# Building the edge matrix of a graph layer in ten blocks of 64 destinations instead of five of 125

## The chip, the core and the metric

The kernel runs on one core of a Trainium2 chip, in one launch. The metric is the time of that launch on the device, in microseconds (us). TensorE multiplies, VectorE (DVE in the profile), ScalarE (ACT) and GpSimd (POOL) work on elements, SyncE (SP) issues most DMAs. Each engine works through its own queue in order and meets the others only through semaphores. A name such as DVEq stands for the queue side of an engine: loading registers from memory, register arithmetic, branches and waits.

## The reference

```python
dst = jnp.minimum((625 * uniform(10000) ** 2.0).astype(int32), 9999)   # then sorted; src follows
edge_index = jnp.stack([src, dst])
xn = _layernorm(x, axis=-1)
x = x + _L0_gnn_ref(xn, edge_index, edge_type_2, ...) + _L0_mix_ref(xn[None], ...)[0]
x = x + _L0_ffn_ref(...)[0]
xn = _layernorm(x, axis=-1)
x = x + _L1_gnn_ref(xn, batch0, edge_index, ...) + _L1_mix_ref(xn[None], ...)[0]
x = x + _L1_ffn_ref(...)[0]
```

There are 625 nodes of 512 features and 10,000 edges of two relations. The change concerns one early stage: from `src`, `dst` and `edge_type_2` the kernel makes a dense matrix of edge counts for each relation, sources by destinations, with which the graph layers later multiply. Since `dst` is the square of a uniform number and sorted, low destinations have many more edges than high ones.

## The kernel before

The edges lie as 80 tiles of 125 edges. For one edge tile VectorE makes two one-hot matrices in 16-bit floats: `oh_src` (125 edges by 625 sources, the `tensor_scalar` of L1171) and `oh_dst` (125 edges by 250 columns, L1172: 125 destinations of relation 0 and 125 of relation 1). TensorE multiplies one by the other (L1712). Destinations are cut in five blocks `j` of `P` = 125; a block has four banks of results (relation 0 and 1, source halves of 312 and 313), so each edge tile takes four matmuls, which accumulate in these banks.

An edge tile is only visited in a block to which it has edges. `EU` = 4 tiles make a group; VectorE first counts which groups each block needs (`pres`, a matmul of ones into the bank `rng`, then small reductions on one partition) and writes first group and number of groups for each block into `rng_i`. VectorE and TensorE then both load these numbers into registers (`value_load`, L1164, L1165 and L1707) and run a loop over groups (`Fori`, L1168 and L1708), written out for the four tiles in it.

The two engines meet in a ring. Each block parity has `EU` slots of `oh_src` and `oh_dst`. VectorE waits for `oh_used{j}` before it writes a slot, and TensorE waits for `oh_ready{j}`; so within a block VectorE can be `EU` tiles ahead. To begin with, the slots of block j+1 are given free when TensorE clears the banks of block j with matmuls of zeros (L1700).

After its loop TensorE closes the banks (L1716). Behind blocks 1, 2 and 3 it does the transposes of the normalised rows (L1650: 16, 16 and 8 matmuls). ScalarE copies the banks into `AT` with a sum for the node degrees (L676). Behind the last block TensorE goes on with the first big product of the mixer (stage `kq`, L1643), and VectorE with the 120 scale-and-add passes over the weight bases (`sum_bases`, L1183 and L1186), which wait for the last block. All order in this stage is written by hand; no planner decides any of it. In the changed kernel the lines of the stage are numbered some 12 higher.

Of the kernel before, what the change touches and what calls it, by code (L numbers as in the profile page):

```python
# [8 lines left out]
P = 125  # L9
# [3 lines left out]
EU = 4  # L13
# [29 lines left out]
PSUM_ORDER = [("rng", 1), ("A0", 8), ("hTa", 4), ("A2", 4), ("hTb", 1), ("xnTa", 3), ("A3", 4), ("xnTb", 2), ("A", 4),  # L43
# [27 lines left out]
A_BLOCK = [("A0", 0), ("A0", 4), ("A2", 0), ("A3", 0), ("A", 0)]  # L71
# [41 lines left out]
def gps_two_layers(nc, I, out):  # L113
# [3 lines left out]
    with ctx:  # L117
# [30 lines left out]
        rng_i = sb("rng_i", [1, 16], i32)  # L148
# [81 lines left out]
        oh_dst = [[ring[:, 876 * u + 626:876 * u + 876] for u in range(EU)] for ring in (oh, oh2)]  # L230
        iota_src = oh[:, 876 * EU:876 * EU + N]
        iota_dst = oh[:, 876 * EU + 626:876 * EU + 876]
        srcf = small[0:P, 0:ET]
        keyf = small[0:P, ET:ET * (1 + TT)].rearrange("p (j t) -> p j t", j=TT)
        dstf, relf = small[0:P, 480:560], small[0:P, 560:640]
        pres, gez = (tmp[0:P, i, 0:TT * ET // 2].bitcast(f16).rearrange("p (j t) -> p j t", j=TT) for i in range(2))
        rank2, held2 = (tmp[0:1, i, 256:256 + 2 * TT * EG].rearrange("p (i j q) -> p i j q", i=2, j=TT) for i in range(2))
        rg = small[0:1, 640:960]
# [301 lines left out]
        def _(pool):  # L540
            step = [0]

            def link(ins):
# [5 lines left out]
            pool.iota(rank2[:, 0, :, :], pattern=[[0, TT], [1, EG]], base=1, channel_multiplier=0, allow_small_or_imprecise_dtypes=True)  # L549
            pool.iota(rank2[:, 1, :, :], pattern=[[0, TT], [-1, EG]], base=EG, channel_multiplier=0, allow_small_or_imprecise_dtypes=True)  # L550
# [22 lines left out]
            pool.iota(iota_dst, pattern=[[1024, 2], [1, P]], base=0, channel_multiplier=0,  # L573
                      allow_small_or_imprecise_dtypes=True).then_inc(S("consts"), 1)
# [75 lines left out]
        def _(act):  # L650
# [46 lines left out]
            def adjacency_out(j):  # L697
                stage, n = A_BLOCK[j]
                for q in range(4):
                    r, (a, w) = q // 2, HALF[q % 2]  # L700
                    copy_out(stage, n + q, AT[:, r, j, a:a + w], B(stage, n + q)[0:P, 0:w], accum_out=deg_part[:, j, q:q + 1])

            adjacency_out(0)
            adjacency_out(1)
# [14 lines left out]
            adjacency_out(2)  # L719
# [3 lines left out]
            adjacency_out(3)  # L723
            for j in range(2):
                xn_columns("xnTb", j, 3 + j)
            adjacency_out(4)
# [320 lines left out]
        def _(dve):  # L1047
# [84 lines left out]
            dve.tensor_copy(pres[:, TT - 1, :], gez[:, TT - 1, :])  # L1132
            dve.tensor_tensor(pres[:, 0:TT - 1, :], gez[:, 0:TT - 1, :], gez[:, 1:TT, :], ALU.subtract).then_inc(S("presence"), 1)
# [5 lines left out]
            rr = rg[:, 0:TT * EG].rearrange("p (j q) -> p j q", j=TT)  # L1139
            rt2 = rg[:, 200:210]  # L1140
            groups_of, first_of = rt2[:, 0:TT], rt2[:, TT:2 * TT]
            most = rg[:, 210:220]
            last, back = most[:, 0:TT], most[:, TT:2 * TT]
# [12 lines left out]
            dve.tensor_copy(rng_i[0:1, 0:10], rt2).then_inc(S("ranges"), 1)  # L1156
# [6 lines left out]
            for j in range(TT):  # L1163
                groups = dve.value_load(rng_i[0:1, j:j + 1], min_val=1, max_val=EG)  # L1164
                q0 = dve.value_load(rng_i[0:1, 5 + j:6 + j], min_val=0, max_val=EG - 1)  # L1165
                if j > 1:
                    dve.wait_ge(S("psum_full"), filled(A_BLOCK[j - 2][0], A_BLOCK[j - 2][1] + 4))
                with dve.Fori(0, groups) as i:  # L1168
                    for u in range(EU):
                        dve.wait_ge(S(f"oh_used{j}"), EU * i + u + 1)  # L1170
                        dve.tensor_scalar(oh_src[j % 2][u], iota_src, small[0:P, bass.ds(EU * q0 + EU * i + u, 1)], None, ALU.is_equal)  # L1171
                        dve.tensor_scalar(oh_dst[j % 2][u], iota_dst, small[0:P, bass.ds(EU * q0 + EU * i + (ET * (j + 1) + u), 1)], None,  # L1172
                                          ALU.is_equal).then_inc(S(f"oh_ready{j}"), 1)
# [465 lines left out]
        def _(pe):  # L1639
# [52 lines left out]
            bk = claim(pe, "rng")  # L1692
            pe.wait_ge(S("presence"), 1)
            group(bk[0:1, 0:TT * ET], [(ones16[0:P, 0:1], pres.rearrange("p j t -> p (j t)"))]).then_inc(S("psum_full"), 1)
            for j in range(TT):
                stage, n = A_BLOCK[j]
                parts = [(B(stage, n + q), q // 2, HALF[q % 2]) for q in range(4)]
                for q, (bkq, r, (a, w)) in enumerate(parts):
                    claim(pe, stage, n + q)
                    ins = pe.matmul(bkq[0:P, 0:w], zero[:, 0:P], zero[:, 0:w], start=True, stop=False)  # L1700
                    if j < TT - 1:
                        ins.then_inc(S(f"oh_used{j + 1}"), 1)
                    if j == 0:
                        pe.matmul(bkq[0:P, 0:1], zero[:, 0:P], zero[:, 0:1], start=False, stop=False).then_inc(S("oh_used0"), 1)
                if j == 0:
                    pe.wait_ge(S("ranges"), 1)
                groups = pe.value_load(rng_i[0:1, j:j + 1], min_val=1, max_val=EG)  # L1707
# [7 lines left out]
                for bkq, r, (a, w) in parts:  # L1715
                    pe.matmul(bkq[0:P, 0:1], zero[:, 0:P], zero[:, 0:1], start=False, stop=True).then_inc(S("psum_full"), 1)  # L1716
# [516 lines left out]
```

## Time and profile before

| what | value |
|---|---|
| median of 3 runs | 808.13 us (807.37 to 809.75) |
| the profiled execution's own time | 807.63 us |
| its span in the profile | 805.9 us |
| TensorE busy | 783.2 us, 97% of the span |
| VectorE busy | 632.0 us, 78% |
| ScalarE busy | 293.2 us, 36% |
| mean granted clock of TensorE | 0.986 of full |

The profiled execution's time is 1.7 us more than its span, for what lies before the first and after the last instruction. Busy times of an engine are of overlapping instructions taken together once; the mean of one matmul is longer than the distance between two, since they are pipelined.

### The profile page before, as it was taken

To read this page: it belongs to the slowest core of one execution; us is meant where nothing else is said; L and a number is where in the kernel's file an instruction comes from. 1 tells how busy PE (TensorE), PEld (TensorE's weight loads), DVE (VectorE), ACT (ScalarE), POOL (GpSimd) and SP (SyncE) were. 2 spreads that over 40 slices of the span, in tenths; PEclk is the share of its full clock that TensorE was granted. 3 is DMA by queue.
4 is the path that set the end of the run, shared out by engine and by line. 5 is a ranking of instruction groups with operands and counts; after the bars stand their busy time and mean duration, and the time that the engine had idled before them with its cause. 6 is when DMAs were issued, how large, how long until landed. Compare 5 with 4: busy or idle time off the path is not lost.

```text
span 805.9 us, 10950 instructions
## 1 busy us (share of the span) xinstructions
PE 783.2 (97%) x3899; PEld 623.4 (77%) x3899; DVE 632.0 (78%) x918; ACT 293.2 (36%) x545; POOL 67.3 (8%) x74
## 2 busy tenths in 40 slices
PE   5999999999999999999999999999999999999997
PEld 4998757867477777477776878897898888888886
DVE  6867999999999999994968454338778865886863
ACT  4453214235411013124142633123445544545541
POOL 3100010220200000000401260030000000000000
PEclk9999999998999999999999999999799999999999
DMA  7600779796898786622041130008133231133101
GB/s 252 239 1 34 228 235 333 247 280 211 249 293 290 245 274 239 229 85 105 0 167 37 70 105 1 1 2 209 53 117 100 71 105 53 53 105 106 53 1 64
DMA packets 68268, 111.67 MB, mean 139 GB/s; under 512 B 4305, under 2 KB 21582, under 8 KB 68220
## 3 DMA queue, kind: packets, MB, share of 16 engines
q1 hardware_dynamic: 62426, 100.51, 37.5%
q0 software_dynamic: 2880, 5.12, 3.7%
q10 hardware_dynamic: 2914, 5.41, 1.8%
q8 instruction: 29, 0.48, 0.2%
q14 instruction: 19, 0.16, 0.1%
HBM read 107.18 MB, written 1.28 MB: 135 GB/s over the span
## 4 chain that ended last, share of the span: by engine, by line
PE 90%; DVE 6%; issue 2%; ACT 1%; DVEq 1%; DMA 0%; SPq 0%; ACTq 0%
PE bank L1643 54%; PE bank L2110 11%; PE bank L1712 6%; PE bank L1862 4%; PE bank L1881 3%; PE bank L1874 2%; PE bank L1855 2%; PE bank L1969 2%; PE bank L1650 2%; PE bank L1761 1%; PE bank L2044 0%; DVE ew_lo L1514 0%; DVE slot L1589 0%; DVE tmp L1099 0%; PE bank L1847 0%
## 5 line engine op out<-in xcount | busy, mean ns | idle before, releaser
L1186 DVE SCALAR_TENSOR_TENSOR weights<-weights,att 128x2048 f32<-128x2048 f32 x116 | 263.4, 2343 | 0.7
L1643 PE MATMUL bank<-half,ew_hi 128*128 128x314 f32 (+1 forms) x456 | 102.8, 314 | 3.3 <-DVE slot L1580 2.0
L1643 PE MATMUL bank<-AT,slot 125*128 125x312 f32 (+1 forms) x400 | 105.8, 426 | 0.0
L1643 PEld LDWEIGHTS bank<-AT,slot 125*128 125x128 f32 x400 | 75.6, 189 | 30.4 <-issue 1.3
L1643 PE MATMUL bank<-weights,slot 128*125 128x512 f32 (+5 forms) x306 | 84.8, 438 | 2.3 <-ACT slot L914 1.6
L1643 PEld LDWEIGHTS bank<-half,ew_hi 128*128 128x128 f32 x456 | 78.5, 193 | 8.1 <-DVE slot L1580 2.8
L1643 PEld LDWEIGHTS bank<-weights,slot 128*125 128x125 f32 (+2 forms) x306 | 50.5, 198 | 30.5 <-issue 26.7
L1643 PE MATMUL bank<-half,ew_lo 128*128 128x314 f32 (+1 forms) x228 | 70.8, 311 | 0.0
L1643 PE MATMUL bank<-slot,weights 128*128 128x313 f32 (+2 forms) x304 | 68.2, 384 | 0.7 <-ACT slot L834 0.7
L676 ACT ACTIVATE slot<-bank 125x512 f32<-125x512 f32 (+7 forms) x62 | 31.2, 538 | 97.6 <-PE bank L1643 87.2
L1643 PEld LDWEIGHTS bank<-slot,weights 128*128 128x128 f32 x304 | 50.9, 193 | 16.8 <-issue 1.3
L2110 PE MATMUL bank<-ew_lo,hid_hi 128*125 128x512 f32 x160 | 63.2, 395 | 0.0
L2110 PE MATMUL bank<-ew_hi,hid_lo 128*125 128x512 f32 x160 | 63.0, 394 | 0.0
L2110 PE MATMUL bank<-ew_hi,hid_hi 128*125 128x512 f32 x160 | 63.0, 394 | 0.0
L1712 PE MATMUL bank<-slot 125*125 125x312 f16 (+1 forms) x384 | 54.2, 303 | 4.6 <-DVE slot L1172 4.5
L1712 PEld LDWEIGHTS bank<-slot 125*125 125x125 f16 x384 | 52.2, 139 | 6.4 <-DVE slot L1172 5.1
L676 ACT ACTIVATE slot<-bank,cols 128x312 f32<-128x312 f32 (+1 forms) x42 | 21.7, 527 | 92.9 <-PE bank L1862 49.0
L1171 DVE TENSOR_SCALAR slot<-slot,small 125x625 f16<-125x625 f16 x96 | 36.8, 383 | 14.7 <-issue 7.8
L970 ACT ACTIVATE slot<-slot,eb_now 128x312 f32<-128x312 f32 (+1 forms) x54 | 29.0, 555 | 50.1 <-DVE slot L1580 27.0
L1643 PEld LDWEIGHTS bank<-half,ew_lo 128*128 128x128 f32 x228 | 43.9, 193 | 0.0
L2110 PEld LDWEIGHTS bank<-ew_hi,hid_lo 128*125 128x125 f32 x160 | 29.7, 185 | 7.4
L2110 PEld LDWEIGHTS bank<-ew_hi,hid_hi 128*125 128x125 f32 x160 | 29.6, 185 | 6.2
(340 smaller groups left out, 1222.7 us busy)
## 6 DMA issues: line engine op xcount, KB each, us to landing
weights<-in_L_gnn_basis SPq DMA_DIRECT2D x60, 1024.0 KB, 5.4
weights<-in_L_ffn_W SPq DMA_DIRECT2D x31, 512.0 KB, 4.4
weights<-in_L_ffn_W SPq DMA_DIRECT2D x16, 256.0 KB, 5.3
weights<-in_L_mix_kqv_w SPq DMA_DIRECT2D x1, 3072.0 KB, 10.3
weights<-in_w_qkvT SPq DMA_DIRECT2D x3, 1024.0 KB, 6.5
slot<-slot POOLq DMA_DIRECT2D x10, 250.0 KB, 7.9
weights<-in_L_mix_mlp_w ACTq DMA_DIRECT2D x2, 1024.0 KB, 17.8
weights<-in_L_gnn_root ACTq DMA_DIRECT2D x2, 1024.0 KB, 10.2
```

Of the source, the lines that this page charges most:

```text
L676: act.activation(dst, src, func, **kw).then_inc(S("act_read"), 1)
L970: act.activation(hid[:, f % 4, a:a + w], hid[:, f % 4, a:a + w], ACT.Silu, bias=eb1_now[:, f:f + 1]).then_inc(S("eh_out"), 1)
L1171: dve.tensor_scalar(oh_src[j % 2][u], iota_src, small[0:P, bass.ds(EU * q0 + EU * i + u, 1)], None, ALU.is_equal)
L1186: ins = dve.scalar_tensor_tensor(wrel[layer][r], wmat(at), att[:, layer, r, b:b + 1], wrel[layer][r], ALU.mult, ALU.add)
L1643: ins = pe.matmul(out, a, b, start=i == 0, stop=i == len(pairs) - 1)
L1650: ins = pe.transpose(bk[:, P * k:P * k + P], src[:, j, 128 * k:128 * k + 128], ident[0:P, 0:P])
L1712: ins = pe.matmul(bkq[0:P, 0:w], oh_dst[j % 2][u][:, P * r:P * r + P], oh_src[j % 2][u][:, a:a + w], start=False, stop=False)
L1855: ins = pe.matmul(bk[:, 0:w], root[0][:, k, 128 * m:128 * m + 128], xnT[:, k, a:a + w], start=k == 0, stop=False)
L1862: ins = pe.matmul(B("h1T", n)[:, 0:w], wrel[0][r][:, k, 128 * m:128 * m + 128], col(Z_AT[r])[:, k, a:a + w], start=False, stop=i == 2 * KT ...
L1874: pe.matmul(bk[0:P, :], h1[:, k, P * j:P * j + P], root[1][:, k, :], start=k == 0, stop=False)
L1881: ins = pe.matmul(B("o2", j)[0:P, :], t[r][:, k, P * j:P * j + P], wt[r][:, k, :], start=False, stop=r == 1 and k == KT - 1 and i == 2)
L2110: ins = pe.matmul(B("eb2", j)[0:P, :], a, b, start=place == 0 and i == 0, stop=place == 15 and i == 2)
```

## The change

Destinations are now cut in ten blocks `b` of 64 and 61 (`BH` = 64; two blocks cover the 125 of one old block). For a block, `oh_dst` has 128 columns: 64 destinations of relation 0 and 64 of relation 1. The product then fills 128 rows of a bank, the lower half for relation 0 and the upper half for relation 1, so a block has two banks and an edge tile two matmuls. ScalarE copies each bank in two pieces, one for each relation. A group has `EU` = 2 tiles, and each ring has 2 slots. The comparison values for the destinations are now made by GpSimd for each block (`iota_dst`, ten small instructions in place of one), so that the five shifted copies of the keys (`keyf`, L1158) go. Semaphore names are shared between blocks b and b+5, so from block 5 on both engines load one more register (`past`, the number of groups of block b-5) and add it to what they wait for.

```diff
-EU = 4
+EU = 2
...
-A_BLOCK = [("A0", 0), ("A0", 4), ("A2", 0), ("A3", 0), ("A", 0)]
+BLOCKS, BH = 2 * TT, 64
+A_BLOCK = [("A0", 0), ("A0", 2), ("A0", 4), ("A0", 6), ("A2", 0), ("A2", 2), ("A3", 0), ("A3", 2), ("A", 0), ("A", 2)]
...
-        oh_dst = [[ring[:, 876 * u + 626:876 * u + 876] for u in range(EU)] for ring in (oh, oh2)]
+        oh_dst = [[ring[:, 876 * u + 626:876 * u + 754] for u in range(EU)] for ring in (oh, oh2)]
...
-            pool.iota(iota_dst, pattern=[[1024, 2], [1, P]], base=0, channel_multiplier=0,
-                      allow_small_or_imprecise_dtypes=True).then_inc(S("consts"), 1)
+            for b in range(BLOCKS):
+                ins = pool.iota(iota_dst[:, b, :], pattern=[[1024, 2], [1, BH]], base=P * (b // 2) + BH * (b % 2), channel_multiplier=0,
+                                allow_small_or_imprecise_dtypes=True)
+            ins.then_inc(S("consts"), 1)
...
-            for j in range(TT):
-                ins = dve.tensor_scalar(gez[:, j, :], dstf, float(P * j), None, ALU.is_ge)
+            for b in range(BLOCKS):
+                ins = dve.tensor_scalar(gez[:, b, :], dstf, float(P * (b // 2) + BH * (b % 2)), None, ALU.is_ge)
...
-            dve.wait_ge(S("psum_full"), filled("rng", 1))
-            cnt = B("rng")[0:1, 0:TT * ET].rearrange("p (j q u) -> p j q u", j=TT, u=EU)
-            dve.tensor_reduce(rr, cnt, AX.X, ALU.add).then_inc(S("rng_out"), 1)
-            dve.wait_ge(S("rng_out"), 1)
+            for i in range(2):
+                dve.wait_ge(S("psum_full"), filled("rng", i + 1))
+                cnt = B("rng", i)[0:1, 0:TT * ET].rearrange("p (b q u) -> p b q u", b=TT, u=EU)
+                dve.tensor_reduce(rr[:, TT * i:TT * i + TT, :], cnt, AX.X, ALU.add).then_inc(S("rng_out"), 1)
+            dve.wait_ge(S("rng_out"), 2)
...
-            for j in range(TT):
-                ins = dve.tensor_scalar(keyf[:, j, :], relf, -float(P * j), None, ALU.add)
-            link(ins)
...
-            for j in range(TT):
-                groups = dve.value_load(rng_i[0:1, j:j + 1], min_val=1, max_val=EG)
-                q0 = dve.value_load(rng_i[0:1, 5 + j:6 + j], min_val=0, max_val=EG - 1)
-                if j > 1:
-                    dve.wait_ge(S("psum_full"), filled(A_BLOCK[j - 2][0], A_BLOCK[j - 2][1] + 4))
+            for b in range(BLOCKS):
+                groups = dve.value_load(rng_i[0:1, b:b + 1], min_val=1, max_val=EG)
+                q0 = dve.value_load(rng_i[0:1, BLOCKS + b:BLOCKS + b + 1], min_val=0, max_val=EG - 1)
+
+                past = dve.value_load(rng_i[0:1, b - TT:b - TT + 1], min_val=1, max_val=EG) if b >= TT else 0
+                if b > 1:
+                    dve.wait_ge(S("psum_full"), filled(A_BLOCK[b - 2][0], A_BLOCK[b - 2][1] + 2))
                 with dve.Fori(0, groups) as i:
                     for u in range(EU):
-                        dve.wait_ge(S(f"oh_used{j}"), EU * i + u + 1)
...
+                        dve.wait_ge(S(f"oh_used{b % TT}"), EU * (past + i) + (u + 1 + (EU if b >= TT else 0)))
+                        dve.tensor_scalar(oh_src[b % 2][u], iota_src, small[0:P, bass.ds(EU * q0 + EU * i + u, 1)], None, ALU.is_equal)
+                        dve.tensor_scalar(oh_dst[b % 2][u], iota_dst[:, b, :], small[0:P, bass.ds(EU * q0 + EU * i + (560 + u), 1)], None,
+                                          ALU.is_equal).then_inc(S(f"oh_ready{b % TT}"), 1)
...
                 with pe.Fori(0, groups) as i:
                     for u in range(EU):
-                        pe.wait_ge(S(f"oh_ready{j}"), EU * i + u + 1)
-                        for bkq, r, (a, w) in parts:
-                            ins = pe.matmul(bkq[0:P, 0:w], oh_dst[j % 2][u][:, P * r:P * r + P], oh_src[j % 2][u][:, a:a + w],
-                                            start=False, stop=False)
-                        ins.then_inc(S(f"oh_used{j}"), 1)
+                        pe.wait_ge(S(f"oh_ready{b % TT}"), EU * (past + i) + (u + 1))
+                        for bkq, a, w in parts:
+                            ins = pe.matmul(bkq[:, 0:w], oh_dst[b % 2][u], oh_src[b % 2][u][:, a:a + w], start=False, stop=False)
+                        ins.then_inc(S(f"oh_used{b % TT}"), 1)
...
-                if j == 1:
+                if b == 3:
                     pe.wait_ge(S("consts"), 1)
                     for i in range(4):
                         tile_to_cols("hTa", i, i, row(3), "h_row")
-                if j == 2:
+                if b == 5:
...
-                if j == 3:
+                if b == 7:
```

```order
L1168 COMPARE_AND_BRANCH
L1164 TENSOR_LOAD rng_i
L1164 ISA x2
L1165 TENSOR_LOAD rng_i
L1165 ISA x2
L1168 UNCONDITIONAL_BRANCH
L1168 ISA
L1171 ISA
L1171 TENSOR_SCALAR slot<-slot,small 125x625
L1172 ISA
L1172 TENSOR_SCALAR slot<-slot,small 125x250
```

The same place in the changed kernel, ahead of block 5 and of each block behind it:

```order
L1180 COMPARE_AND_BRANCH
L1174 TENSOR_LOAD rng_i
L1174 ISA x2
L1175 TENSOR_LOAD rng_i
L1175 ISA x2
L1177 TENSOR_LOAD rng_i
L1177 ISA x2
L1180 UNCONDITIONAL_BRANCH
L1180 ISA
L1183 ISA
L1183 TENSOR_SCALAR slot<-slot,small 125x625
L1184 ISA
```

A third register load has come in (ahead of blocks 1 to 4 there are still two), and there are nine such places in place of four.

On TensorE, the last tile of a group of four and the close of a block before:

```order
L1710 REGISTER_ALU
L1712 MATMUL bank<-slot 125x312
L1712 MATMUL bank<-slot 125x313
L1712 MATMUL bank<-slot 125x312
L1712 MATMUL bank<-slot 125x313
L1708 REGISTER_ALU
L1708 COMPARE_AND_BRANCH
L1716 MATMUL bank<-zero 125x1 x4
```

In the changed kernel, a whole group and the close of a block:

```order
L1728 MATMUL bank<-slot 128x312
L1728 MATMUL bank<-slot 128x313
L1726 REGISTER_ALU
L1728 MATMUL bank<-slot 128x312
L1728 MATMUL bank<-slot 128x313
L1724 REGISTER_ALU
L1724 COMPARE_AND_BRANCH
L1731 MATMUL bank<-zero 128x1 x2
```

A tile has two matmuls in place of four, and the branch of the loop stands behind every second tile in place of every fourth.

## Rows read from the trace of the kernel before

**Rows 1.** The page: span, and the granted clock of TensorE in 40 slices.

```profile
span 805.9 us, 10950 instructions
...
PEclk9999999998999999999999999999799999999999
```

**Rows 2.** The chain that ended last, in order of time: start us, us, what.

```profile
8.97 0.55 DVEq L1164
11.53 20.23 PE bank L1712 x136
...
44.74 0.32 PE bank L1716 x4
45.06 1.86 PE bank L1650 x16
46.92 0.67 PE bank L1700 x4
...
67.76 6.62 PE bank L1712 x48
74.38 0.32 PE bank L1716 x4
74.70 69.38 PE bank L1643 x258
```

**Rows 3.** Groups by line, 10.8 to 74.7 us: count, busy us, mean ns, idle before.

```profile
L1712 PE MATMUL bank<-slot 125*125 125x312 f16 (+1 forms) x384 | 54.2, 303 | 4.6 <-DVE slot L1172 4.5
...
L1171 DVE TENSOR_SCALAR slot<-slot,small 125x625 f16<-125x625 f16 x96 | 36.8, 383 | 14.7 <-issue 7.8 <-PE bank L1712 5.5
L1172 DVE TENSOR_SCALAR slot<-slot,small 125x250 f16<-125x250 f16 x96 | 27.0, 281 | 0.0
```

**Rows 4.** Timeline, VectorE in block 1: start us, us, instruction.

```profile
35.65 0.28 DVE L1172 TENSOR_SCALAR slot<-slot,small 125x250 f16<-125x250 f16 x1
35.84 0.38 DVE L1171 TENSOR_SCALAR slot<-slot,small 125x625 f16<-125x625 f16 x1
36.13 0.28 DVE L1172 TENSOR_SCALAR slot<-slot,small 125x250 f16<-125x250 f16 x1
```

**Rows 5.** Timeline, TensorE: first matmuls of block 1, and of block 2.

```profile
35.98 0.61 PE L1712 MATMUL bank<-slot 125*125 125x312 f16 x3
```

```profile
47.57 0.61 PE L1712 MATMUL bank<-slot 125*125 125x312 f16 x3
```

**Rows 6.** Timeline, VectorE: the turn from block 1, and block 2's fifth tile.

```profile
43.09 0.29 DVE L1172 TENSOR_SCALAR slot<-slot,small 125x250 f16<-125x250 f16 x1
44.73 0.39 DVE L1171 TENSOR_SCALAR slot<-slot,small 125x625 f16<-125x625 f16 x1 [1.34 <-issue]
...
48.54 0.39 DVE L1171 TENSOR_SCALAR slot<-slot,small 125x625 f16<-125x625 f16 x1 [1.77 <-PE bank L1712]
```

**Rows 7.** The chain, 33 to 60 us: one register load of VectorE's queue.

```profile
34.34 0.30 DVEq L1165
...
34.67 0.20 DVEq L1165
...
34.96 0.04 DVEq L1168
```

**Rows 8.** Groups by line and shape on VectorE, 0 to 10.8 us.

```profile
L1130 DVE TENSOR_SCALAR tmp<-small 125x80 f16<-125x80 f32 x5 | 0.9, 236 | 0.0
L1158 DVE TENSOR_SCALAR small<-small 125x80 f32<-125x80 f32 x5 | 0.8, 249 | 0.0
L1146 DVE TENSOR_REDUCE small<-bank 1x100 f32<-1x400 f32 x1 | 0.6, 561 | 0.0
...
L1151 DVE TENSOR_REDUCE small<-tmp 1x10 f32<-1x200 f32 x1 | 0.3, 349 | 0.0
L1133 DVE TENSOR_TENSOR tmp<-tmp 125x320 f16<-125x320 f16 x1 | 0.3, 320 | 0.0
```

**Rows 9.** Line L1712 from 11.5 to 15.2 us: ns min/median/max.

```profile
L1712 PE MATMUL bank<-slot x14: 464/468/521, 11.5 to 15.0; 125*125 125x312 f16 x7, 125*125 125x313 f16 x7
```

**Rows 10.** The same line from 36 to 44.8 us.

```profile
L1712 PE MATMUL bank<-slot x64: 293/296/347, 36.0 to 44.4; 125*125 125x312 f16 x32, 125*125 125x313 f16 x32
```

**Rows 11.** Busy time by window: each engine, granted clock, DMA share, GB/s.

```profile
162.10:165.60 3.50, 3.50 (x23) 2.54 (x21) 3.50 (x3) 1.57 (x2) 0.00 (x0) 1.00 1.03 278
```

```profile
175.80:179.20 3.40, 3.40 (x34) 1.00 1.10 266
179.20:182.60 3.40, 3.40 (x19) 0.50 1.05 258
```

**Rows 12.** Groups on TensorE in the first of those windows, and in the second.

```profile
L1643 PE MATMUL bank<-weights,slot 128*128 128x512 f32 x5 | 2.3, 592 | 0.0
L1643 PE MATMUL bank<-small,slot 128*125 128x1 f32 x18 | 2.0, 244 | 0.0
```

```profile
L1643 PE MATMUL bank<-gate_w,slot 128*125 128x2 f32 x34 | 4.0, 251 | 0.0
```

**Rows 13.** Busy time of all engines, 75 to 145 us, columns as above.

```profile
75.00:145.00 70.00, 70.00 (x265) 48.59 (x264) 68.74 (x38) 20.93 (x38) 4.61 (x5) 1.00 0.82 261
```

More of the change, by code:

```diff
@@ L229, in gps_two_layers @@
         oh_src = [[ring[:, 876 * u:876 * u + N] for u in range(EU)] for ring in (oh, oh2)]
-        oh_dst = [[ring[:, 876 * u + 626:876 * u + 876] for u in range(EU)] for ring in (oh, oh2)]
+        oh_dst = [[ring[:, 876 * u + 626:876 * u + 754] for u in range(EU)] for ring in (oh, oh2)]
         iota_src = oh[:, 876 * EU:876 * EU + N]
-        iota_dst = oh[:, 876 * EU + 626:876 * EU + 876]
+        iota_dst = weights[0:P, 4096:4736].bitcast(f16).rearrange("p (b d) -> p b d", b=BLOCKS)
         srcf = small[0:P, 0:ET]
-        keyf = small[0:P, ET:ET * (1 + TT)].rearrange("p (j t) -> p j t", j=TT)
         dstf, relf = small[0:P, 480:560], small[0:P, 560:640]
-        pres, gez = (tmp[0:P, i, 0:TT * ET // 2].bitcast(f16).rearrange("p (j t) -> p j t", j=TT) for i in range(2))
-        rank2, held2 = (tmp[0:1, i, 256:256 + 2 * TT * EG].rearrange("p (i j q) -> p i j q", i=2, j=TT) for i in range(2))
-        rg = small[0:1, 640:960]
+        pres, gez = (tmp[0:P, i, 0:BLOCKS * ET // 2].bitcast(f16).rearrange("p (b t) -> p b t", b=BLOCKS) for i in range(2))
+        rank2, held2 = (weights[0:1, 4736 + 800 * i:4736 + 800 * i + 2 * BLOCKS * EG].rearrange("p (i b q) -> p i b q", i=2, b=BLOCKS)
+                        for i in range(2))
+        rg = weights[0:1, 6336:6336 + BLOCKS * EG + 4 * BLOCKS]
         AT0 = AT[:, 0, :, :].rearrange("p j s -> p (j s)")
@@ L696, in _, with adjacency_out @@
                 act.activation(row(3)[:, j, :], xn[:, j, :], ACT.Copy, scale=hv[:, j:j + 1]).then_inc(S("h_row"), 1)
[L697 to L704, printed above, removed]
+            def adjacency_out(b):
+                stage, n = A_BLOCK[b]
+                j, at, rows = b // 2, BH * (b % 2), (BH, P - BH)[b % 2]
+                for hf, (a, w) in enumerate(HALF):
+                    act.wait_ge(S("psum_full"), filled(stage, n + hf + 1))
+                    for r in range(2):
+                        ins = act.activation(AT[at:at + rows, r, j, a:a + w], B(stage, n + hf)[BH * r:BH * r + rows, 0:w], ACT.Copy,
+                                             accum_out=deg_part[at:at + rows, j, 2 * r + hf:2 * r + hf + 1])
+                    ins.then_inc(S("act_read"), 1)
+            for b in range(4):
+                adjacency_out(b)
             act.wait_ge(S("cols_in"), 16)
@@ L718, in _ @@
                 h_columns("hTa", j, j)
-            adjacency_out(2)
+            adjacency_out(4)
+            adjacency_out(5)
             h_columns("hTb", 0, 4)
@@ L1691, in _ @@
             pe.wait_ge(S("first_consts"), 1)
-            bk = claim(pe, "rng")
             pe.wait_ge(S("presence"), 1)
[L1694 to L1705, printed above, removed]
+            for i in range(2):
+                bk = claim(pe, "rng", i)
+                group(bk[0:1, 0:TT * ET], [(ones16[0:P, 0:1], pres[:, TT * i:TT * i + TT, :].rearrange("p b t -> p (b t)"))])\
+                    .then_inc(S("psum_full"), 1)
@@ new lines, in _ @@
+            for b in range(BLOCKS):
+                stage, n = A_BLOCK[b]
+                parts = [(B(stage, n + hf), a, w) for hf, (a, w) in enumerate(HALF)]
+                for hf, (bkq, a, w) in enumerate(parts):
+                    claim(pe, stage, n + hf)
+                    ins = pe.matmul(bkq[:, 0:w], zero[:, 0:128], zero[:, 0:w], start=True, stop=False)
+                    if b < BLOCKS - 1:
+                        ins.then_inc(S(f"oh_used{(b + 1) % TT}"), EU // 2)
+                    if b == 0:
+                        pe.matmul(bkq[:, 0:1], zero[:, 0:128], zero[:, 0:1], start=False, stop=False).then_inc(S("oh_used0"), EU // 2)
+                if b == 0:
@@ L1718, in _ @@
+                for bkq, a, w in parts:
+                    pe.matmul(bkq[:, 0:1], zero[:, 0:128], zero[:, 0:1], start=False, stop=True).then_inc(S("psum_full"), 1)
+                if b == 3:
                     pe.wait_ge(S("consts"), 1)
```

38 lines of the change are left out of this document (18 added, 20 removed).

## Prediction, before the changed kernel was run

> **What bounds the kernel now.** I read the page first [rows 1]: the span is 805.9 us and TensorE's granted clock is near full nearly everywhere, so this is a kernel that lives by TensorE's matmuls. Then the chain that ended last [rows 2], over the stage that the change touches. The reader is to see that it holds nothing but TensorE from 11.53 us, when block 0's first matmul starts, to 74.70 us, when the `kq` product starts: matmuls of L1712, closing matmuls, transposes, clearing matmuls. Behind 74.70 us the chain is TensorE again; there VectorE begins its base sums at the same event, and both are full: from 75 to 145 us TensorE is busy 70.00 and VectorE 68.74 of 70 us [rows 13]. No transfer is awaited there. So whatever moves the end of this stage moves all that follows, one for one.
>
> Next I asked how near VectorE is to TensorE in the stage. By line [rows 3] there are 384 matmuls for 96 tiles, and TensorE idles only before the very first. In block 1, 64 matmuls start within 36.0 to 44.4 us [rows 10], 0.134 us apart, so a tile takes 0.535 us. VectorE starts an `oh_src` 0.29 us before its `oh_dst` and an `oh_dst` 0.19 us before the next `oh_src` [rows 4]: 0.48 us for a tile. It has 14.7 us of idle time before L1171 [rows 3]. The two engines are thus within 10% of each other; with four slots in the ring the matmuls set the pace and the handshake is hidden.
>
> **What the change does, part by part.** *Matmuls.* The blocks' groups, counted from the sorted destinations of the input, are 13, 7, 5, 4, 4, 4, 3, 3, 3, 3: 49 groups of two, 98 tiles in place of 96. So 196 matmuls replace 384, and 188 of 0.134 us are 25.2 us less TensorE work. That is a gain only as far as TensorE still sets the pace.
>
> *The handshake in a ring of two.* Within a block VectorE may write tile t+2 only when TensorE has finished tile t. That is a closed loop, and each leg has a row. From `oh_src` start to `oh_dst` start 0.29 us [rows 4]. The `oh_dst` itself took 0.28 us for 250 columns; L1171 with 625 columns took 0.38 us, so a column is 0.27 ns, and 128 columns make 0.25 us. From its end at 35.93 us to the first matmul at 35.98 us is 0.05 us [rows 4, 5]. Three matmuls that meet an idle TensorE take 0.61 us [rows 5]; less one distance of 0.134 us, two take 0.48 us. From the end of a tile's last matmul to VectorE's next start: block 2's first matmul starts at 47.57 us, its fourth ends 0.61 + 0.134 us later, at 48.31, and `oh_src` of the fifth tile, which waited for it, starts at 48.54 us [rows 5, 6]: 0.23 us. The loop is 0.29 + 0.25 + 0.05 + 0.48 + 0.23 = **1.30 us, say 1.31, for two tiles**. TensorE is busy 0.53 us of it, VectorE's datapath 2 x (0.48 - 0.03) = 0.90 us. Neither is the bound: the loop is. The 25 us saved on TensorE turn into waiting.
>
> *The turn from block to block.* VectorE's last `oh_dst` of block 1 starts at 43.09 us and the first `oh_src` of block 2 at 44.73 us [rows 6]: 1.64 us, with two register loads. A third load costs 0.62 us (34.34 to 34.96 us) [rows 7], so the turn is 2.26 us from block 5 on. In a group the second `oh_dst` starts 0.45 + 0.29 = 0.75 us behind the group's first `oh_src`, so a turn makes the group 2.39 or 3.01 us long in place of 1.31: 1.09 more, or 1.71. Nine turns are 4 x 1.09 + 5 x 1.71 = 12.9 us. Before, these turns were covered, because TensorE had up to four tiles of 0.535 us in hand; now it has two of 0.27 us.
>
> *Transposes.* They stay on TensorE, at three turns. From the last matmul of block 1 to the first of block 2 there are 3.13 us (start 44.44 to 47.57) [rows 2, 5, 10]. The VectorE path of a turn, counted from the last matmul, is 1.76 or 2.38 us. With sixteen transposes TensorE is the later one by 1.37 us, twice (its own third register load adds to the second as VectorE's does), and with eight by 0.54: 3.3 us.
>
> *The start.* VectorE makes ten comparisons in place of five (0.9 us for five [rows 8], so 0.8 more), a subtraction over 720 in place of 320 columns (0.32 us; between nothing and 0.4 more, I take 0.2), a second reduction of 400 counts (0.56), two products and a reduction on one partition over four times as many elements. 400 elements took 0.56 and 200 took 0.35 us [rows 8], about 1.05 ns each, so 2 x 0.31 + 0.63. The five shifted keys go, 0.8 us. That is 2.0 us later: the first `oh_src` at 12.9 us. GpSimd's ten small comparison rows are done before that.
>
> *ScalarE, DMAs.* 40 bank copies replace 20, four in a block of at least 4 us; if one were late it would be the last block's, whose banks `kq` does not take first. At nothing. No DMA is added or moved; the `kqv` weights have long landed.
>
> **The sum.** End of the stage: 12.9 (start) + 49 x 1.31 = 64.2 + 12.9 (turns) + 3.3 (transposes) + 0.4 (the last group's matmuls and the close, less what 1.31 holds) = 93.7 us, against 74.70 us. That is 19.0 us later, with TensorE at full clock throughout.
>
> *The clock.* At first the matmuls take 468 ns, at 1.2 GHz [rows 9]; at full clock, 2.4 GHz, 296 ns [rows 10]. The clock rose after TensorE had streamed without a gap. It stayed full in a stretch where about half of TensorE's time went to one-column matmuls and half to long ones, and fell behind one of two-column matmuls alone [rows 11, 12]. Now TensorE streams 0.53 of 1.31 us, less in the last blocks, which lies between. At half clock the two matmuls of the loop take 0.26 + 0.47 = 0.73 in place of 0.48 us, 0.25 more for each of 49 groups: 12 us at most. I take 2 us, for a later rise and a slow stretch near the end.
>
> The Trainium skill warns in "TensorE: Matmul & The Clock Gate" (A second HAM failure mode) that a TensorE which pauses briefly between groups of matmuls can have its clock go up and down, at a cost in throughput. No stretch of this trace shows such short regular pauses; by that rule the rival of half clock below is the likelier one.
>
> So +21 us. On the profiled execution's own time that is 807.63 + 21 = 828.6 us; the median of the runs is 0.5 us above it, so 829.
>
> **The rivals.**
> *The clock stays at half for the whole stage* (chance 0.17). For it: from the start TensorE never streams without gaps. Against: at half clock it streams 1.04 of 1.56 us, and two blocks stay long. 19 + 12 = 31 us, 839 us.
> *The queue of VectorE sets the pace, not the ring* (0.08): TensorE answers faster than the rows of a waking engine say. Then a group costs between its datapath's 0.90 us and 1.31; a branch behind every second tile speaks for about 1.08. 49 x 0.23 = 11.3 us less: about +8, 816 us.
> *Faster* (0.05): VectorE runs ahead and its datapath is the pace, so that the matmuls removed show. It is decided by the length of a group. The end comes before 74.70 us only if 12.9 + 49p + 12.9 + 3.3 + 0.4 is less, p under 0.92 us. At 0.90 that is -1 us; if the turns were hidden behind queued work too, up to -12: I put it at -6, 802 us. Against it: the ring has two slots, and the turn is VectorE's own queue.
> *No change* (0.03): something later takes the delay up, a transfer or a sum that was late anyway. Against it: the chain behind 74.70 us is TensorE without gaps.
> *The forecast, the ring's loop at mostly full clock* (0.67): 824 to 834 us.
>
> **Range and chances.** The forecast and the half clock hold 0.84; the range reaches from 818 (the forecast's loop 0.2 us shorter, 10 us less, to which the queue rival comes near) to 840 us. About 0.3% is what a measurement of this kernel tells from no change. Faster 0.05, within 0.3% 0.03, slower 0.92.
>
> **What would show it.** `kq`'s first matmul at about 94 to 96 us. TensorE idle before L1728 for over 30 us, nearly all put down to VectorE's L1184, where it was 4.6. VectorE idle before L1183 put down to TensorE in nearly every group, with consecutive groups 1.3 us apart in block 0. Turns of 1.6 and 2.3 us on VectorE. The first `oh_src` at 12.9 us. Behind `kq` the same distances as before. Wrong if groups are 1.1 us or less apart, if matmuls of 468 ns fill the stage, or if the time behind `kq` shrinks.

## The result, and the profile after

The changed kernel took 840.2 us (median of 4 runs, 839.5 to 840.5) against 807.8 us (807.4 to 809.8) for the kernel before: 1.0394 times as long, 95% interval 1.0378 to 1.041. The profiled execution took 840.39 us with a span of 838.6 us.

The page, with span and the granted clock in 40 slices; to be set against [rows 1]:

```profile
span 838.6 us, 10819 instructions
...
PEclk9997689999899999999999999999979999999999
```

The chain that ended last, in order of time (start us, us, what); to be set against [rows 2]:

```profile
10.95 0.54 DVEq L1174
13.48 0.72 PE bank L1728 x2
15.02 0.72 PE bank L1728 x2
16.56 0.72 PE bank L1728 x2
...
60.72 3.53 PE bank L1662 x16
...
77.70 3.53 PE bank L1662 x16
...
92.24 1.86 PE bank L1662 x8
...
105.33 71.54 PE bank L1655 x258
```

Where there was one piece of 136 matmuls in 20.23 us, there are now pieces of two matmuls that begin 1.54 us apart. `kq` begins at 105.33 us in place of 74.70. The span grew by 32.7 us, and the chain says where:

- The first matmul starts at 13.48 in place of 11.53 us: 2.0 us.
- From there to `kq` it takes 91.85 in place of 63.17 us: 28.7 us.
- The first 258 matmuls of `kq` take 71.54 in place of 69.38 us: 2.2 us.
- Behind them the distances are those of before: together these three are already 32.8 us.

Groups by line, 10 to 108 us (count, busy us, mean ns, idle us before and what ended it); to be set against [rows 3]:

```profile
L1728 PE MATMUL bank<-slot 125*128 125x312 f16 x196 | 57.6, 436 | 25.7 <-DVE slot L1184 25.5
L1183 DVE TENSOR_SCALAR slot<-slot,small 125x625 f16<-125x625 f16 x98 | 37.8, 385 | 44.0 <-PE bank L1728 25.8 <-issue 9.6 <-PE bank L1731 4.3
L1184 DVE TENSOR_SCALAR slot<-weights,small 125x128 f16<-125x128 f16 x98 | 24.3, 248 | 0.0
```

Both engines wait, each for the other. TensorE is idle 25.5 us for VectorE's `oh_dst`, where it was 4.5 (all of the 4.5 lay ahead of the first matmul; 6.1 of the 25.5 do). VectorE is idle 25.8 us for TensorE's matmuls, where it was 5.5. This is what a closed loop looks like: no engine is full, and each names the other. The second thing to see is the mean of one matmul, 436 ns in place of 303: half of the matmuls are gone, and the busy time of TensorE on this line rose from 54.2 to 57.6 us.

Timeline of VectorE in block 0:

```profile
12.88 0.39 DVE L1183 TENSOR_SCALAR slot<-slot,small 125x625 f16<-125x625 f16 x1 [1.97 <-issue]
...
14.42 0.39 DVE L1183 TENSOR_SCALAR slot<-slot,small 125x625 f16<-125x625 f16 x1 [0.54 <-PE bank L1728]
...
15.95 0.39 DVE L1183 TENSOR_SCALAR slot<-slot,small 125x625 f16<-125x625 f16 x1 [0.53 <-PE bank L1728]
```

Groups are 1.54 us apart, with a wait for TensorE in each. The next four views are of L1728, 13 to 33, 33 to 60, 66 to 72 and 73 to 77 us (ns min/median/max), and answer to [rows 9, 10]:

```profile
L1728 PE MATMUL bank<-slot x52: 440/468/468, 13.5 to 32.7; 125*128 125x312 f16 x26, 125*128 125x313 f16 x26
```

```profile
L1728 PE MATMUL bank<-slot x64: 440/468/468, 32.7 to 59.8; 125*128 125x313 f16 x32, 125*128 125x312 f16 x32
```

```profile
L1728 PE MATMUL bank<-slot x13: 297/307/308, 66.3 to 71.9; 125*128 125x312 f16 x7, 125*128 125x313 f16 x6
```

```profile
L1728 PE MATMUL bank<-slot x12: 441/468/468, 72.6 to 76.8; 125*128 125x313 f16 x6, 125*128 125x312 f16 x6
```

By these durations block 0 ran at 1.2 GHz to its end, and so did all up to 60 us, where before [rows 9] only the first 3.5 us did. The windows (from:to, length, busy us of PE, PEld, DVE, ACT and POOL with counts, granted clock, DMA share, GB/s):

```profile
33.00:60.00 27.00, 21.46 (x76) 5.61 (x76) 16.28 (x64) 6.44 (x24) 0.00 (x0) 1.00 0.07 24
66.00:72.00 6.00, 3.19 (x17) 0.96 (x18) 3.44 (x15) 4.70 (x16) 0.00 (x0) 1.00 0.00 0
73.00:82.00 9.00, 8.16 (x34) 4.51 (x34) 3.72 (x16) 4.20 (x14) 0.00 (x0) 0.50 0.01 2
83.00:89.00 6.00, 3.06 (x16) 0.85 (x16) 3.06 (x13) 2.08 (x8) 0.00 (x0) 1.00 0.01 1
90.00:105.00 15.00, 12.16 (x47) 4.41 (x44) 7.02 (x28) 5.42 (x18) 0.00 (x0) 0.50 0.00 0
```

From 66 us on, the granted clock and the durations agree: 307 ns at 1.00, 468 ns at 0.50. Before that they don't. From 33 to 60 us the granted clock reads 1.00 although the matmuls take the same 468 ns as at 0.50, and it reads 1.00 in the 468 ns stretch of [rows 9] too. No stretch at 0.50 stands in this trace before 72 us. So at the head of a trace I go by the durations; the first slices of the line PEclk, and the mean clock of a run, read too high for this stage.

The clock came up twice, each time behind sixteen transposes and the clearing matmuls (60.72 and 77.70 us in the chain), and fell again after some 7 us of pairs of matmuls with gaps. Behind the eight transposes at 92.24 us it did not come up. `kq` itself began at half clock (0.50 from 105 to 107 us, 1.00 again before 120 us), which is its 2.2 us.

### The profile page after: what moved, and what is told of

The parts are those of the page before. It is cut to its first block, busy times and chain, and to the rows that moved or that the text cites. A ratio compares the mean times of both kernels' runs of the same rounds, so it can differ in the third digit from the quotient of the medians.

```text
span 838.6 us, 10819 instructions
## 1 busy us (share of the span) xinstructions
PE 794.0 (95%) x3710; PEld 589.1 (70%) x3710; DVE 634.1 (76%) x923; ACT 306.2 (37%) x585; POOL 69.3 (8%) x83
## 4 chain that ended last, share of the span: by engine, by line
PE 85%; DVE 7%; issue 3%; DVEq 2%; ACT 1%; DMA 0%; SPq 0%; ACTq 0%
PE bank L1655 52%; PE bank L2125 11%; PE bank L1877 4%; PE bank L1728 4%; PE bank L1896 3%; PE bank L1889 2%; PE bank L1662 2%; PE bank L1870 2%; PE bank L1984 2%; DVE slot L1184 1%; DVEq L1183 1%; PE bank L1776 1%; DVE slot L1183 0%; PE bank L2059 0%; DVE slot L1601 0%
## 5 line engine op out<-in xcount | busy, mean ns | idle before, releaser
L1728 PE MATMUL bank<-slot 125*128 125x312 f16 x196 | 57.6, 436 | 25.7 <-DVE slot L1184 25.5
L1655 PE MATMUL bank<-slot,weights 128*128 128x313 f32 (+2 forms) x304 | 70.5, 393 | 0.7 <-ACT slot L846 0.7
L1183 DVE TENSOR_SCALAR slot<-slot,small 125x625 f16<-125x625 f16 x98 | 37.8, 385 | 44.0 <-PE bank L1728 25.8
L1728 PEld LDWEIGHTS bank<-slot 125*128 125x128 f16 x196 | 15.5, 116 | 67.3 <-DVE slot L1184 65.6
L681 ACT ACTIVATE slot<-bank,cols 128x312 f32<-128x312 f32 (+1 forms) x42 | 21.8, 526 | 94.1 <-PE bank L1877 49.0
L708 ACT ACTIVATE AT<-bank 64x312 f32<-64x312 f32 (+3 forms) x40 | 17.1, 426 | 47.5 <-PE bank L1731 47.0
```

The costliest lines, as they stand in the source:

```text
L681: act.activation(dst, src, func, **kw).then_inc(S("act_read"), 1)
L708: ins = act.activation(AT[at:at + rows, r, j, a:a + w], B(stage, n + hf)[BH * r:BH * r + rows, 0:w], ACT.Copy, accum_out=deg_part[at:at + ...
L1183: dve.tensor_scalar(oh_src[b % 2][u], iota_src, small[0:P, bass.ds(EU * q0 + EU * i + u, 1)], None, ALU.is_equal)
L1655: ins = pe.matmul(out, a, b, start=i == 0, stop=i == len(pairs) - 1)
L1728: ins = pe.matmul(bkq[:, 0:w], oh_dst[b % 2][u], oh_src[b % 2][u][:, a:a + w], start=False, stop=False)
```

## The experiments

Theories: **the ring** (two slots close a loop of 1.31 us for a group), **the clock** (how much of the loss is the half clock), and the rival that TensorE or VectorE alone sets the pace. Each run is compared with the kernel before on the same chip.

**e4_before_ring2: the kernel before, with two of its four slots.** Everything else stays: 96 tiles, four matmuls each, five blocks.

```diff
-                        dve.wait_ge(S(f"oh_used{j}"), EU * i + u + 1)
-                        dve.tensor_scalar(oh_src[j % 2][u], ...
+                        dve.wait_ge(S(f"oh_used{j}"), EU * i + u + 3)
+                        dve.tensor_scalar(oh_src[j % 2][u % 2], ...
```

> The kernel before, with only two of its four slots used in each ring; groups, blocks and four matmuls stay. My loop gives (0.30 + 0.28 + 0.05 + 0.75 + 0.15 or 0.23) 1.53 to 1.61 us for two tiles in place of 1.07, so the product behind the stage starts at about 95 us in place of 74.7: 828 to 830 us, at full clock, since TensorE streams 1.07 of it. At half clock it would be 850 us. If the ring is not what costs, no change: 808 us.

Measured: 829.69 us, 1.0265 times the kernel before (1.0244 to 1.0286). `kq` began at 97.56 us, 2.6 us later than I had expected. Timeline, 20 to 24 us, and the line view, 17 to 43 us:

```profile
20.99 1.29 PE L1712 MATMUL bank<-slot 125*125 125x312 f16 x8 [0.25 <-DVE slot L1172]
...
21.96 0.39 DVE L1171 TENSOR_SCALAR slot<-slot,small 125x625 f16<-125x625 f16 x1 [0.49 <-PE bank L1712]
...
22.60 1.28 PE L1712 MATMUL bank<-slot 125*125 125x312 f16 x8 [0.32 <-DVE slot L1172]
...
23.50 0.39 DVE L1171 TENSOR_SCALAR slot<-slot,small 125x625 f16<-125x625 f16 x1 [0.47 <-PE bank L1712]
```

```profile
L1712 PE MATMUL bank<-slot x134: 293/297/432, 16.6 to 43.0; 125*125 125x313 f16 x67, 125*125 125x312 f16 x67
```

Two tiles take 1.61 and 1.53 us in turn, with a gap on either engine, where they took 1.07 us. The work is the same and 22 us are lost: two slots fewer are enough for a loss of the size that I forecast for the whole change. Here the clock stayed full (297 ns) through 26 us in which TensorE paused 0.25 or 0.32 us behind every eighth matmul. This stage had begun with 5.5 us of matmuls without a gap; the changed kernel paused from its fifth matmul on.

**e1_group4: the changed kernel with groups and rings of four.** The ring is undone in the changed kernel; the blocks are then padded to 116 tiles.

```diff
-EU = 2
+EU = 4
```

> One part of the change undone: groups and rings of four tiles, in the ten blocks of 64. The blocks then visit 116 tiles in place of 98. If the ring of two slots is what costs (my theory), a tile costs VectorE's own 0.46 to 0.50 us in place of 0.77, the TensorE clock comes back, and the product behind the stage starts at 83 to 90 us in place of 105.3: 815 to 825 us in all. If the register loads and branches of VectorE's queue were the cost and the ring not, the 18 extra tiles come on top and the time stays at 835 us or more.

Measured: 817.01 us, 1.0106 (1.0079 to 1.0133), with `kq` at 82.19 us. The row of VectorE in the stage (10 to 125 us):

```profile
L1183 DVE TENSOR_SCALAR slot<-slot,small 125x625 f16<-125x625 f16 x116 | 44.4, 383 | 16.4 <-issue 8.7 <-PE bank L1662 3.7 <-PE bank L1731 3.2
```

The wait for L1728, 25.8 us in the changed kernel, has gone from VectorE's row. With 18 tiles more it is 23.2 us faster than the changed kernel. Some of that is not the loop: its clock was higher too, and its first matmul started at 12.26 in place of 13.48 us. There are half as many groups to count, and part of the 1.2 us is chance (see e3_no_third_load).

**e3_no_third_load: `past` is kept in the register of the block five earlier**, on both engines.

```diff
-                past = dve.value_load(rng_i[0:1, b - TT:b - TT + 1], min_val=1, max_val=EG) if b >= TT else 0
+                past = seen[b - TT] if b >= TT else 0
```

> The changed kernel without the third register load from block 5 on, in both queues: the number of groups of block b-5 is kept in the register that it was loaded to. My price is 0.62 us for each of five turns, 3.1 us, less what transposes hide: 837 us. If loads are covered by other waits: 840 us.

Measured: 835.53 us, 1.0345 (1.0325 to 1.0366), 4.7 us less than the changed kernel. The same edit on top of e1_group4 (**e6_group4_kept_registers**):

> Groups and rings of four in ten blocks, and no third register load from block 5 on. With a ring of four VectorE sets the pace, so each of the five loads should come off in full: 3.1 us under the run with groups of four alone, 814 us, or up to 4.5 us as in the run without the load. If the ring of four hides the turns, no difference: 817 us.

Measured: 814.37 us, 1.0068 (1.0045 to 1.0091), 2.6 us less than e1_group4, though the runs of the two overlap (811.6 to 815.0 and 814.6 to 817.8 us). The forecast price was 3.1 us, which lies between the two.

The traces say what the 4.7 us are. `kq` began 4.9 us earlier than in the changed kernel (100.42 us). The five turns with a third load took 12.5 in place of 15.3 us, from a group's first `oh_src` to the next group's: 2.8 us, near the 3.1. The first `oh_src` started 0.44 us earlier, ahead of any third load, and mostly because L1148, which is the same instruction in both, took 0.20 in place of 0.48 us: that is no effect of the edit. The clock also came up a third time (matmuls of 306 ns from 91 to 98 us), and groups there took 1.3 in place of 1.6 us: about the size of the rest.

**e2_one_filler: a matmul of zeros behind each tile, one row deep,** so that TensorE has less idle time. It adds nothing to the result.

```diff
                         ins.then_inc(S(f"oh_used{b % TT}"), 1)
+                        pe.matmul(bkq[:, 0:w], zero[:, 0:128], zero[:, 0:w], start=False, stop=False)
```

> The changed kernel, and behind each edge tile one more matmul of zeros over 313 columns into the same bank, which adds nothing to it. It gives TensorE work where it waited. If waiting is what holds the clock at 1.2 GHz, the clock rises in the stage, groups of two come 1.31 us apart in place of 1.54, and the stage ends near 94 us: 827 to 830 us. If the clock is no matter of how much TensorE streams, or a matmul of zeros does not count, the group stays at 1.54 us or longer: 840 us or more.

Measured: 860.26 us, 1.064 (1.0616 to 1.0665), 20 us more than the changed kernel. Timeline of TensorE, and the filler's row of the line view (14 to 98 us, ns min/median/max):

```profile
20.07 0.70 PE L1728 MATMUL bank<-slot 125*128 125x312 f16 x2
20.71 0.44 PE L1730 MATMUL bank<-zero 1*128 1x313 f16 x1
21.08 0.70 PE L1728 MATMUL bank<-slot 125*128 125x312 f16 x2
21.72 0.44 PE L1730 MATMUL bank<-zero 1*128 1x313 f16 x1
22.09 0.70 PE L1728 MATMUL bank<-slot 125*128 125x312 f16 x2
```

```profile
L1730 PE MATMUL bank<-zero x74: 436/437/438, 13.7 to 94.1; 1*128 1x313 f16 x74
```

TensorE has hardly any idle time by these records, and yet it stays at half clock: the filler takes 437 ns from 13.7 to 94.1 us. Behind the sixteen transposes that follow, the chain has it at 0.24 in place of 0.37 us for a while: what brought the clock up was not the filler. A tile takes 1.01 us, and now TensorE is the bound. A tile's pair is 0.70 us long when nothing overlaps it, and 0.37 us pass from filler to pair, so the one-row matmul is hardly overlapped with its neighbours. As a test of the clock this failed, since the filler neither raised it nor fitted into the gaps.

**e5_full_filler: the same with 125 rows.** The stationary matrix is the ones, the moving one 313 columns of zeros that GpSimd fills. It adds nothing to the result.

```diff
+            pool.memset(zeros_in, 0.0)
...
+                        pe.matmul(bkq[0:P, 0:w], ones16[0:P, :], zeros_in[:, 0:w], start=False, stop=False)
```

> The changed kernel with a filler matmul behind each tile as in the run with one filler, but with 125 rows on both sides: a constant matrix of ones times 313 columns of zeros, so that nothing is added and weights of one row never alternate with weights of 125. In the last filler run each filler stood 0.14 us away from the matmuls on both sides. If that gap came with the one-row weights, it goes, and three matmuls take 0.78 us at half clock without a gap; the clock should then rise, the groups come 1.31 us apart, and the stage end near 94 us: 827 to 830 us. If the clock stays at half all the same, a group is 1.56 us: 840 to 843 us.

Measured: 826.69 us, 1.0239 (1.0215 to 1.0264). With 98 matmuls more than the changed kernel it is 13.5 us faster. L1730 of this kernel, 20 to 64 us; VectorE's timeline; and the chain at `kq`:

```profile
L1730 PE MATMUL bank<-slot x116: 296/299/308, 20.1 to 63.9; 125*128 125x312 f16 x58, 125*128 125x313 f16 x58
```

```profile
20.80 0.39 DVE L1185 TENSOR_SCALAR slot<-slot,small 125x625 f16<-125x625 f16 x1 [0.27 <-PE bank L1730]
...
22.07 0.41 DVE L1185 TENSOR_SCALAR slot<-slot,small 125x625 f16<-125x625 f16 x1 [0.27 <-PE bank L1730]
...
23.37 0.39 DVE L1185 TENSOR_SCALAR slot<-slot,small 125x625 f16<-125x625 f16 x1 [0.27 <-PE bank L1730]
```

```profile
93.47 69.38 PE bank L1657 x258
```

At full clock a group takes 1.27 to 1.30 us; VectorE still waits for TensorE in each. `kq` begins at full clock and takes its old 69.38 us. Two things qualify the comparison. The first four groups (1.55 to 1.57 us) and some of the late ones were still at half clock. And the first `oh_src` started at 12.29 in place of 12.88 us, ahead of any filler.

**e10_group4_filler: e6_group4_kept_registers with this filler.**

> Ten blocks, groups and rings of four, kept registers, and the filler matmul with 125 rows behind each tile. TensorE's work is then 0.40 us of a tile's 0.49 us, so VectorE still sets the pace, but the clock should stay full where it went up and down without the filler. Its slow windows cost some 2 to 3 us in the stage and none behind it: 811 to 813 us. If the clock does not matter once VectorE sets the pace: 814 us.

Measured: 813.42 us, 1.0055 (1.0037 to 1.0073). 1 us less than without, and the two runs' ranges (811.2 to 814.1 and 811.6 to 815.0 us) lie over each other. The windows 16 to 79 us of the two, without the filler and with it:

```profile
16.00:79.00 63.00, 56.47 (x291) 23.19 (x290) 49.90 (x213) 38.87 (x116) 3.46 (x5) 0.87 0.29 102
```

```profile
16.00:79.00 63.00, 58.26 (x406) 35.06 (x404) 50.60 (x216) 39.11 (x116) 4.45 (x5) 1.00 0.30 105
```

And VectorE in the run with the filler:

```profile
19.25 0.38 DVE L1187 TENSOR_SCALAR slot<-slot,small 125x625 f16<-125x625 f16 x1
19.54 0.25 DVE L1188 TENSOR_SCALAR slot<-weights,small 125x128 f16<-125x128 f16 x1
19.70 0.38 DVE L1187 TENSOR_SCALAR slot<-slot,small 125x625 f16<-125x625 f16 x1
```

The clock went from 0.87 to 1.00 and the time did not follow. With four slots the tiles come 0.45 us apart and VectorE has no gap between them: inside a block it sets the pace. So the matmuls that the change takes away, and the speed at which the rest run, are hidden behind it.

**e7_before_fewer_tiles: the kernel before with fewer tiles.** Groups are counted in pairs, the loop of fours is followed by a loop of one or two pairs, and both engines load one register more (VectorE a third, TensorE a second): 88 tiles in place of 96.

```diff
-EU = 4
+EU = 2
+RU = 4
...
+                more = dve.value_load(rng_i[0:1, 10 + j:11 + j], min_val=1, max_val=2)
...
+                with dve.Fori(0, more) as i:
```

> The kernel before, five blocks and rings of four, but blocks may begin at every second tile: a loop over groups of four and a short loop of one or two pairs behind it. 88 tiles are visited in place of 96, eight times 0.535 us less on TensorE: 4.3 us. On VectorE a turn costs one more load, 0.62 us, and a second loop entry, and the start is some 1.3 us later by eight small operations. Where TensorE still sets the pace the time is 805 to 806 us. If VectorE's turns come out from under TensorE, they cost what is gained: 807 to 809 us.

Measured: 809.58 us, 1.001 (0.9997 to 1.0022). No gain: the first matmul started at 13.60 us in place of 11.53, behind the finer count and the third load. `kq` began 1.8 us later than before, at 76.49 us, so from the first matmul to `kq` only 0.3 us was won by eight tiles fewer.

**e9_before_early_start: a shorter start, alone.** Comparison rows for each block from GpSimd and no `keyf`, which is the one part of the change that shortens the start; and, which the change does not have, no load of `q0` for block 0, which is always zero.

```diff
-            for j in range(TT):
-                ins = dve.tensor_scalar(keyf[:, j, :], relf, -float(P * j), None, ALU.add)
-            link(ins)
...
+                q0 = dve.value_load(rng_i[0:1, 5 + j:6 + j], min_val=0, max_val=EG - 1) if j else 0
+                if j == 1:
+                    dve.wait_ge(S("first_consts"), 2)
```

> The kernel before with the one part of the change that shortens the way to the first tile: comparison values for each block from GpSimd, so that the five shifted keys (0.8 us) go; and block 0 begins at tile 0 without a register load (0.62 us). The first matmul comes 1.3 us earlier and all else follows: 806.5 us. If something else is awaited at the start (GpSimd's constants), 807.5 us.

Measured: 806.54 us, 0.998 (0.9965 to 0.9996): 1.3 us less. The chain:

```profile
8.69 0.55 DVEq L1167
10.52 22.94 PE bank L1717 x160
```

The first matmul started 1.0 us earlier than in [rows 2], not 1.3 as expected.

**e8_before_90_tiles: both together, with no third load and no second loop.** The loop of fours is followed by one pair written out straight, which makes 90 tiles, and the start is that of e9.

```diff
                 with dve.Fori(0, groups) as i:
+                    for u in range(RU):
+                        one_hot_tile(i, u)
+                for u in range(2):
+                    one_hot_tile(groups, u)
```

> The kernel before with 90 tiles in place of 96 and no dearer turn: blocks begin at every second tile, the loop takes groups of four, and one pair of tiles stands as straight code behind it, so no load and no second loop. The start is as in the run with the earlier start below, but for 0.5 us longer counts on one partition and two more small operations. Six tiles of 0.535 us are 3.2 us, the start about 0.5 us earlier: 804 us. If VectorE's turns come out from under TensorE all the same, 806 to 807 us.

Measured: 804.44 us, 0.9947 (0.993 to 0.9964), faster than both kernels. Its chain, of an execution that took 806.65 us, the longest of its six:

```profile
11.54 23.19 PE bank L1726 x152
...
72.27 69.38 PE bank L1657 x258
```

`kq` begins 2.4 us earlier than before. None of that is the start: the first matmul came at 11.54 us, as in [rows 2], so the finer count took back about what e9 had won, and the 0.5 us expected of it did not show. Here six tiles fewer do count (3.2 us by the old distance of two tiles), since TensorE is still the bound and nothing was added to VectorE's turns.

## Why the prediction was right, and which term was not

**The time.** The 840.2 us are 11 us above the forecast of 829 and outside the 824 to 834 us of the case that had a chance of 0.67. They lie at the very end of the range (818 to 840). What came is the rival of the half clock, which had 0.17. One of the forecast's own signs of being wrong was met: matmuls of 468 ns fill the stage. Others were missed for the same reason: `kq` at 105.33 and not at 94 to 96 us, groups of 1.54 and not 1.3 us, TensorE idle before L1728 for 25.7 and not over 30 us, since slower matmuls fill more of each gap.

**The mechanism of the ring was right.** The loop of the ring of two is shown from both sides: e4_before_ring2 puts it into the old kernel and loses 22 us, e1_group4 takes it out of the new one and gains 23 us. The 25 us of matmuls that the change removes bought nothing, because neither engine was the bound any more; at four slots it is VectorE, as the timeline of e10_group4_filler shows. So the rivals in which VectorE's queue or its datapath sets the pace, and with them "faster", are out for the ring of two.

**The sum at full clock held.** The first `oh_src` was forecast for 12.9 us and started at 12.88; a match to 0.02 us is luck, for in e2_one_filler and e3_no_third_load, with the same instructions up to there, it started at 12.42 and 12.44. A group was forecast at 1.31 us at full clock, and took 1.27 to 1.30 in e5_full_filler; at half clock 1.56, and took 1.54. The turns: 1.66 us with two loads (forecast 1.64), and with three loads 2.26 us (forecast 2.26). Their rows in the timeline of the changed kernel, first with two loads, then with three:

```profile
32.09 0.25 DVE L1184 TENSOR_SCALAR slot<-weights,small 125x128 f16<-125x128 f16 x1
33.75 0.39 DVE L1183 TENSOR_SCALAR slot<-slot,small 125x625 f16<-125x625 f16 x1 [1.42 <-issue]
```

```profile
69.01 0.24 DVE L1184 TENSOR_SCALAR slot<-weights,small 125x128 f16<-125x128 f16 x1
71.27 0.39 DVE L1183 TENSOR_SCALAR slot<-slot,small 125x625 f16<-125x625 f16 x1 [2.01 <-issue]
```

The end of the stage was put at 93.7 us "with TensorE at full clock throughout"; e5_full_filler, which is at full clock for most of the stage, has it at 93.47 us. This is no exact proof: it started 0.6 us earlier and its groups were up to 0.04 us shorter than forecast, while some of them ran at half clock. These errors pull in opposite directions.

**The term that failed is the clock**: "I take 2 us, for a later rise and a slow stretch near the end." TensorE was at half clock for all but two stretches of about 7 us. The stage ended at 105.33 and not at 93.7 us, 11.6 us later, and VectorE's timeline says where (distances between the first `oh_src` of one group and of the next, against the terms of the forecast):

| part | forecast us | measured us | more |
|---|---|---|---|
| 36 groups without turn or transposes | 47.2 | 54.8 | 7.6 |
| 3 groups in which TensorE transposes | 7.2 | 10.7 | 3.4 |
| 9 turns | 24.7 | 25.0 | 0.3 |
| the last group and the close | 1.7 | 2.0 | 0.3 |

So the half clock cost 7.6 us in the groups, and 3.4 us in the transposes, which the prediction had priced at full clock: sixteen of them took 3.53 us where they took 1.86 before [rows 2], and eight took 1.86 us. The turns are VectorE's own time and hardly changed. To this comes a cost that I had not thought of in either case: `kq` began at half clock and lost 2.2 us. Together with the 11.6 us that is 13.8 us; e5_full_filler was 13.5 us faster than the changed kernel, of which 0.6 us is its earlier start.

The rival of the half clock (839 us) came within about 1 us of the result, and that is luck. It charged 0.25 us to each of 49 groups, 12 us, though the turns do not lengthen and some groups ran at full clock, and it had neither the slower transposes nor the slow start of `kq`. The two errors cancel.

What misled me was the weighing of [rows 11, 12]: they bracket TensorE's share of work, but by stretches in which it streams without a break, and the new stage is made of short work and regular gaps. None of the rows read before the run had such a stretch, and the two ends of the bracket gave no reason to sit near the one that I chose.

The Trainium skill, "TensorE: Matmul & The Clock Gate", A second HAM failure mode, says that brief idle times between groups of matmuls can make the clock go up and down. The changed kernel agrees (granted clock 0.50 in 73 to 82 and in 90 to 105 us, 1.00 in 83 to 89 us), and more: by its 468 ns the clock was down for most of the stage. e4_before_ring2 does not: it paused as regularly and kept matmuls of 297 ns for 26 us. So brief pauses alone don't decide it. Beside a trace that could not decide either, the rule of the Trainium skill should have had more than a small chance.

**Smaller terms.** The third load at 3.1 us: 2.8 us in the turns of e3_no_third_load (on TensorE the added load is its second, not its third as the prediction has it). ScalarE and DMAs at nothing: the three pieces of the chain already hold the whole loss. Behind `kq` the same distances as before: from the end of the first 258 matmuls on, that was so.

## What to carry to other kernels

When a ring between two engines gets shorter, write down the closed loop (both engines' work on a slot, and the two answers between them) and compare it with each engine's own time; if it is longer, work taken from either engine is worth nothing. Then ask what the new gaps do to TensorE's clock: here its price was about 13 of the 32.7 us, it is paid by everything that TensorE does in the stage, and the start of the next stage lost 2.2 us to it. If the gaps can't be closed, full-depth matmuls of zeros put into them are a cheap trial, but only where TensorE is on the path: with two slots they won 13.5 us, with four 1 us, within the scatter of the runs.

## What the runs showed of the hardware that I had not expected

- Less work made TensorE busier: 196 matmuls at a mean of 436 ns in place of 384 at 303 ns. Adding 98 idle ones of 125 rows brought the mean of these 196 to 331 ns (299 ns at the median from 20 to 64 us) and the kernel from 840.2 to 826.7 us.
- Fillers of one row did not do this. They left TensorE at half clock to 94 us with hardly a gap in its records, and a tile of pair and filler took 1.01 us. Whether it is the one row that kept the clock down, or small gaps between matmuls of different depth that the records don't show, was not settled.
- Pauses alone do not hold the clock down. With two slots the old kernel paused 0.25 to 0.32 us behind every eighth matmul and kept 297 ns; the changed kernel paused 0.31 us behind every fourth and stayed at 468 ns. What tips it between these two was not settled.
- A value in memory costs VectorE's queue about 0.6 us to load. Kept in a register over five blocks it made five turns 2.8 us shorter in all, with no cost that could be seen.
- The granted clock read 1.00 for the first 60 us of the changed kernel while its matmuls took 468 ns. The durations are the surer witness at the head of a trace.
